# Second MLP in tiles of 128 tokens with another order of the norm; both MLPs with five up-products of 128 rows

## The reference, cut to what matters

```
x  = x + proj(attention(layernorm(x)))                       # first block
x  = x + (gelu(layernorm(x) @ mlp_w1 + mlp_b1) @ mlp_w2 + mlp_b2)

h  = irfft2(filter(rfft2(layernorm(x)))) + layernorm(x)      # second block
h  = h + x
m  = gelu(layernorm(h) @ fc1_w + fc1_b) @ fc2_w + fc2_b      # 192 -> 768 -> 192
out = m + h
```

## Time and profile before

| | |
|---|---|
| median of 3 runs | 1118.7 us (1117.19 to 1119.45) |
| profiled execution | 1113.0 us, its span 1111.2 us |
| mean granted TensorE clock | 0.959 of full |
| busy: TensorE, VectorE, ScalarE, GpSimd | 1033.5 (93%), 847.2 (76%), 700.6 (63%), 170.7 us (15%) |
| chain that ended last, by engine | PE 71%, DVE 12%, DMA 7%, ACT 5%, issue 3%, POOL 2% |
| down-products, 864 | 77.5 us busy |
| up-products, 432 | 75.0 us busy |

### The profile page before, as it was taken

One profiled execution on the slowest core, in us unless ns is written; L12 is line 12 of the kernel. 1 busy time (PEld: TensorE's weight loads), 2 busy tenths in 40 slices (PEclk: granted clock), 3 DMA queues, 4 the chain that ended last, 5 costly groups with the idle time before them and its releaser, 6 DMA issues.

```text
span 1111.2 us, 35967 instructions
## 1 busy us (share of the span) xinstructions
PE 1033.5 (93%) x15606; PEld 731.5 (66%) x15606; DVE 847.2 (76%) x1714; ACT 700.6 (63%) x1003; POOL 170.7 (15%) x142
## 2 busy tenths in 40 slices
PE   5867889999999999999999999999989889998998
PEld 3545246665777776677776767676657776775776
DVE  4837978889999999999999999999526764233443
ACT  4646157677787777777777877777865442231554
POOL 4430000910000000000000000000024544001443
PEclk9885579999999999999999999999999999999999
DMA  4698967657474756565656566554400001211110
GB/s 122 172 223 271 239 119 167 107 99 129 85 121 93 111 97 107 96 107 101 103 100 105 104 99 108 96 95 88 80 13 21 25 23 34 68 54 41 40 45 23
DMA packets 83011, 109.17 MB, mean 98 GB/s; under 512 B 14109, under 2 KB 75234, under 8 KB 82661
## 3 DMA queue, kind: packets, MB, share of 16 engines
q1 hardware_dynamic: 82853, 106.87, 48.9%
HBM read 85.40 MB, written 21.44 MB: 96 GB/s over the span
## 4 chain that ended last, share of the span: by engine, by line
PE 71%; DVE 12%; DMA 7%; ACT 5%; issue 3%; POOL 2%; SPq 0%; DVEq 0%; ACTq 0%; POOLq 0%
PE ps L1028 35%; PE ps L1189 17%; PE ps L1023 15%; DVE mx_p L1485 4%; DVE xh L101 2%; POOL rstd L109 1%; DMA m_d<-mneg 1%; DVE stage_lo L1454 1%; PE ps L1041 1%; ACT hid_f L955 1%; DVE stats L88 1%; DMA rel_d<-stage_lo 1%; DMA rel<-in_c_rel_w 1%; PE ps L1135 1%; DMA qv<-m_d 1%
## 5 line engine op out<-in xcount | busy, mean ns | idle before, releaser
L1485 DVE TENSOR_REDUCE mx_p<-ps 128x1 f32<-128x464 f32 (+1 forms) x1080 | 608.6, 629 | 34.4 <-PE ps L1028 23.2
L905 ACT ACTIVATE prob<-ps 128x768 f32<-128x768 f32 x648 | 496.2, 810 | 184.9 <-PE ps L1028 184.1
L1028 PE MATMUL ps<-kc,qc 112*32 112x464 f16 (+1 forms) x4320 | 460.4, 370 | 8.6 <-issue 4.4
L1028 PE MATMUL ps<-qv,ka 113*32 113x384 f16 x5184 | 403.8, 328 | 10.3 <-DMA qv<-m_d 7.7
L1189 PE MATMUL ps<-prob,v_ext 128*32 128x384 f32 x2592 | 293.3, 487 | 2.5 <-issue 2.0
L1028 PEld LDWEIGHTS ps<-qv,ka 113*32 113x32 f16 x5184 | 213.9, 97 | 86.7 <-issue 28.6
L1028 PEld LDWEIGHTS ps<-kc,qc 112*32 112x32 f16 x4320 | 173.2, 95 | 108.0 <-DVE mx_p L1485 30.0
L1189 PEld LDWEIGHTS ps<-prob,v_ext 128*32 128x32 f32 x2592 | 117.0, 111 | 17.4 <-issue 3.2
L1023 PE MATMUL ps<-w_dn,hid 128*96 128x192 f16 x864 | 77.5, 249 | 6.6 <-DVE hid L1540 4.4
L1023 PEld LDWEIGHTS ps<-w_dn,hid 128*96 128x96 f16 x864 | 73.2, 125 | 12.0 <-issue 6.1
L752 POOL COPY v_ext<-v_all 128x288 f32<-128x288 f32 x12 | 5.1, 427 | 480.6 <-PE ps L1189 480.5
(11 more groups left out here) (106 smaller groups left out, 838.2 us busy)
## 6 DMA issues: line engine op xcount, KB each, us to landing
qv<-rel_d SPq DMA_DIRECT2D x216, 144.0 KB
qv<-kq_d SPq DMA_DIRECT2D x108, 216.0 KB
qc<-rel_d SPq DMA_DIRECT2D x24, 216.0 KB, 4.0
xin<-in_x SPq DMA_DIRECT2D x12, 288.0 KB, 3.3
kq_d<-khl SPq DMA_DIRECT2D x24, 144.0 KB, 2.3
q_h<-kq_d SPq DMA_DIRECT2D x9, 288.0 KB, 4.7
q_w<-qw_d SPq DMA_DIRECT2D x9, 288.0 KB, 6.7
rel_d<-stage_hi SPq DMA_DIRECT2D x4, 648.0 KB, 7.6
```

The lines of the kernel that those rows point to most:

```text
L905: nc.scalar.activation(prob[:, s4(p, s), :].rearrange("p (a b) -> p a b", a=2), ps[:, 3 + 2 * (s % 2):5 + 2 * (s % 2), 0:CW], ACT.Exp).the ...
L1028: ins = nc.tensor.matmul(ps[c:c + 32, bank, 0:w], l[:, c:c + 32], r, start=True, stop=True, tile_position=(0, c))
L1485: nc.vector.tensor_reduce(mx_p[:, q * GT + k // MP, k % MP:k % MP + 1], ps[:, slot, 0:min(MW, N - k % MP * MW)], AX, ALU.max).then_inc(uni ...
```

## The change

Both MLPs: the channels are cut in 128 and 64, not 96 and 96. The high and the low part of the 64 channels are stacked in one piece of 128 rows (x[:, 2, :]), and the weight rows of these channels are loaded twice, so that two products of 128 rows (w high, w low) give all four of their combinations. An up tile is then 5 products: 3 for the 128 channels and 2 for the 64. ScalarE and VectorE each take two instructions for the parts of x instead of one. gain, shift and the weights w_up have 128 partitions; gain and shift of each norm are loaded by two DMAs, so that 4 loads come to `load_weights`, and `load_mlp` has one more load each.

Second MLP alone: `down` works in three tiles of 128 tokens (54 products) instead of four of 96 (72). x3 is written in tiles of 96 tokens, so SP stores it to memory and reads it back as x3t in tiles of 128 (`to_wide_tiles`); GpSimd adds the bias there (`bias_into_wide`), VectorE writes y_o in two instructions. The inverse transform of the next chunk comes before the up-products, the transposes before the wait for the low parts, GpSimd's rstd after two hid tiles, not four, and VectorE's two hid tiles after xh.

```diff
@@ -331,12 +336,12 @@
...
-            load(eng, gain[1][:, :], d["L0_conv_ln2_g"].rearrange("(k p) -> p k", p=C2))
-            load(eng, shift[1][:, :], d["L0_conv_ln2_b"].rearrange("(k p) -> p k", p=C2))
-            load(eng, gain[2][:, :], d["L1_conv_g2"].rearrange("(k p) -> p k", p=C2))
-            load(eng, shift[2][:, :], d["L1_conv_be2"].rearrange("(k p) -> p k", p=C2))
+            for dst, nm in ((gain[1], "L0_conv_ln2_g"), (shift[1], "L0_conv_ln2_b"),
+                            (gain[2], "L1_conv_g2"), (shift[2], "L1_conv_be2")):
+                load(eng, dst[:, 0:1], d[nm][0:128].rearrange("(p o) -> p o", o=1))
+                load(eng, dst[0:C - 128, 1:2], d[nm][128:C].rearrange("(p o) -> p o", o=1))
...
@@ -631,7 +636,9 @@
...
-                sp.dma_start(w_up_f[i][:, :, :], d[up].rearrange("(k p) n -> p k n", p=C2)).then_inc(w_mlp_in, 16)
+                sp.dma_start(w_up_f[i][:, 0, :], d[up][0:128, :]).then_inc(w_mlp_in, 16)
+                sp.dma_start(w_up_f[i][:, 1, :], d[up][128:C, :].unsqueeze(0).to_broadcast([2, C - 128, HID]))\
+                  .then_inc(w_mlp_in, 16)
...
@@ -693,15 +700,27 @@
...
+            def to_wide_tiles(c):
+                rows_c = x3_d[c * CW:(c + 1) * CW, :]
+                sp.wait_ge(x3_ok, c + 1)
+                sp.dma_start(rows_c.rearrange("(t p) c -> p t c", p=T), x1[:, ds(c * CT, CT), :]).then_inc(x3_out, 16)
+                sp.wait_ge(x3_out, 16 * (c + 1))
+                sp.dma_start(x3t[:, c % 2, :, :], rows_c.rearrange("(j p) c -> p j c", p=128))\
+                  .then_inc(x3t_in[c % 2], 16)
...
+                if more:
+                    to_wide_tiles(c + 1)
...
@@ -806,14 +825,19 @@
...
+            def bias_into_wide(c):
+                pool.wait_ge(x3t_in[c % 2], 16 * (c // 2 + 1))
+                x = x3t[:, c % 2, :, :]
+                nc.gpsimd.tensor_tensor(x, x, rows[:, 3:4, :].to_broadcast([128, 3, C]), ALU.add).then_inc(x3b_ok, 1)
+
             def block1(c, more):
-                lo_of_hidden(c, up1, range(POOL_TILES))
+                bias_into_wide(c)
+                lo_of_hidden(c, up1, range(2))
                 if more:
                     norm_root(pool, nc, rstd, ln4, c + 1)
-                    bias_into(c + 1, 3, ln4, x3b_ok)
+                lo_of_hidden(c, up1, range(2, POOL_TILES))
...
@@ -889,12 +913,14 @@
...
+                x = chunk_of(xnt_all, c)
+                for k, m in enumerate((128, C - 128)):
...
-                nc.scalar.activation(chunk_of(xnt_all, c)[:, :, 0, :], xnt_f[:, :, :], ACT.Copy).then_inc(x_hi, 1)
+                nc.scalar.activation(x[:, 0, :], xnt_f[:, 0, :], ACT.Copy)
+                nc.scalar.activation(x[0:C - 128, 2, :], xnt_f[0:C - 128, 1, :], ACT.Copy).then_inc(x_hi, 1)
...
@@ -1247,15 +1277,15 @@
...
-                    for k in range(2):
-                        for part in range(2):
-                            mm(ps[:, m % 2, 0:CW], w_up[i][:, k, part, m * 128:(m + 1) * 128], x[:, k, 0, :],
-                               start=(k == 0 and part == 0), stop=False)
+                    w, o = w_up[i][:, :, :, m * 128:(m + 1) * 128], ps[:, m % 2, 0:CW]
+                    mm(o, w[:, 0, 0, :], x[:, 0, :], stop=False)
+                    mm(o, w[:, 0, 1, :], x[:, 0, :], start=False, stop=False)
 
                 def lo_products(m):
-                    for k in range(2):
-                        ins = mm(ps[:, m % 2, 0:CW], w_up[i][:, k, 0, m * 128:(m + 1) * 128], x[:, k, 1, :],
-                                 start=False, stop=(k == 1))
+                    w, o = w_up[i][:, :, :, m * 128:(m + 1) * 128], ps[:, m % 2, 0:CW]
+                    mm(o, w[:, 0, 0, :], x[:, 1, :], start=False, stop=False)
+                    mm(o, w[:, 1, 1, :], x[:, 2, :], start=False, stop=False)
+                    ins = mm(o, w[:, 1, 0, :], x[:, 2, :], start=False)
...
@@ -1272,31 +1302,36 @@
...
+                W, late = (T, (1, 3)) if i == 0 else (128, (1,))
...
-                            mm(down_tile(t), hid[:, m, 0, t * T:(t + 1) * T], w_dn[i][:, part, m, :],
+                            mm(down_tile(t), hid[:, m, 0, t * W:(t + 1) * W], w_dn[i][:, part, m, :],
...
                 for tiles in (range(HM - 2), range(HM - 2, HM - 1), range(HM - 1, HM)):
                     pe.wait_ge(sems["hi"], c * HM + tiles.stop)
                     for t in (0, 2):
                         hi_products(t, tiles)
+                if i == 1:
+                    half_way()
                 pe.wait_ge(sems["lo"], (c + 1) * HM)
                 for t in (0, 2):
                     lo_products(t)
-                half_way()
-                for t in (1, 3):
+                if i == 0:
+                    half_way()
+                for t in late:
                     hi_products(t, range(HM))
                     ins = lo_products(t)
                 ins.then_inc(sems["dn_ps"], 1)
...
@@ -1401,7 +1436,9 @@
...
-                up(c, 1, up1, {2: lambda: inverse_w(c + 1)} if more else {})
+                if more:
+                    inverse_w(c + 1)
+                up(c, 1, up1, {})
                 down(c, 1, up1, lambda: norm_transposed(c + 1, ln4, t4_ps) if more else None)
...
@@ -1460,7 +1497,9 @@
...
-                nc.vector.tensor_tensor(x[:, :, 1, :], xnt_f[:, :, :], x[:, :, 0, :], ALU.subtract).then_inc(x_lo, 1)
+                nc.vector.tensor_tensor(x[:, 1, :], xnt_f[:, 0, :], x[:, 0, :], ALU.subtract)
+                nc.vector.tensor_tensor(x[C - 128:128, 2, :], xnt_f[0:C - 128, 1, :], x[0:C - 128, 2, :],
+                                        ALU.subtract).then_inc(x_lo, 1)
...
@@ -1589,17 +1628,27 @@
...
             def block1(c, more):
                 tiles = range(POOL_TILES, HM)
                 if more:
-                    inverse(c + 1, lambda: lo_of_hidden(c, up1, tiles))
-                else:
-                    lo_of_hidden(c, up1, tiles)
-                mlp_sum(c, up1, x3b_ok, lambda: wait_used(dve, y_out, 16 * c))
+                    inverse(c + 1, lambda: None)
+                lo_of_hidden(c, up1, tiles)
+                if more:
+                    lo_of_input(c + 1, 1)
+                dve.wait_ge(up1["dn_ps"], c + 1)
+                dve.wait_ge(x3b_ok, c + 1)
...
+                nc.vector.scalar_tensor_tensor(out=y[:, 0:2 * C], in0=ps[:, 2, 0:2 * C], scalar=1 / WS,
+                                               in1=x3[:, 0:2 * C], op0=ALU.mult, op1=ALU.add)
```

65 lines of the change are left out of this document (40 added, 25 removed).

## The result

The changed kernel takes 1138.62 us (median, 1137.73 to 1140.65), the kernel before 1117.95 us in the same session: ratio 1.0204, 95% interval 1.0170 to 1.0237. I had forecast 1118.5, so it is 20.1 us slower than forecast and above the range. The profiled execution of it took 1137.73 us with a span of 1135.9, that of before 1113.01 with 1111.2.

What follows compares the result with a forecast made beforehand. TensorE was taken to bound the second MLP, a chain through VectorE the first. The terms 1.9 - 1.7 + 1.1 + 0 - 2.3 + 0.8 = -0.2 us, added to 1118.7, gave 1118.5; range 1109 to 1125.

Steps and rivals of the forecast that it cites:

- Constants, +1.9: Second head: four more small loads in SP's queue, ahead of the qv loads, cost 1.9 us (bounds 0 and +2.5).
- The bigger w_up_f load: Beside attention: the larger up-weight load costs 0, as no row shows TensorE waiting for it.
- First MLP, -1.7: First MLP: -0.2 us for each of four rounds, chunk 0 gains 0.5, the last chunk 0.4; bounds +1.0 and -3.5.
- Start of the second MLP, +1.1: Second MLP's start: x3's store and read-back before u2's load delay the first up-product by 1.1 us; bounds 0.2 and 2.
- A steady chunk, 14.35: Second MLP: rounds of 14.35 us against 14.34, xh waiting on GpSimd instructions; 0 over five rounds, bounds -8.7 and +1.5.
- Last chunk, -2.3: Second MLP's last chunk, no norm beside it: fewer down-products give -2.1, with the two y_o instructions -2.3 us.
- Clock, +0.8: TensorE's longer waits in the first MLP and new ones in the second: half of one more half-clock stretch, +0.8 us.
- rival C: Second MLP: half-clock stretches of 3.3 us after TensorE's new wait, 1.7 us each, +4.1 in all, 1122.8; chance 0.17.
- A: Second MLP: TensorE and ScalarE bound throughout, the lock hurts little, rounds of 12.6 us, -9.7 in all, 1109; chance 0.13.
- B: Second MLP: x3's round trip lasts past 9.1 us, so the bias misses xh; rounds of 13.35, -6.0, 1112.7; chance 0.15.
- D: Second head: the constants cost nothing, SP's delay being absorbed; -2.1 us in all, 1116.6; chance 0.10.

Runs made afterwards that it cites:

- e2: e1 with the four short gain and shift loads moved from the second head to the sixth; 1127.95 us, ratio 1.0083 to the kernel before.
- e1: The changed kernel with the one broadcast transfer of up-weight rows 128 to 192 written as two plain transfers of 64 rows; 1132.09 us, ratio 1.0124.
- e8: The kernel before plus one broadcast transfer of up-weight rows in the first head, into a tile nobody reads; 1120.33 us, ratio 1.0051.
- e9: e4 with the first MLP of the kernel before; 1109.62 us, ratio 0.9922.
- e5: e4 with the first product of each up tile in the first MLP run twice; 1117.26 us, ratio 1.0016.
- e10: e4 with short loads spread over heads 4 to 7; in the first MLP's last chunk GpSimd's tiles after xh, VectorE's before h; 1111.60 us, ratio 0.9960.
- e12: e1 with ten products nobody reads in TensorE's wait for xh in each second-MLP chunk; 1126.42 us, ratio 1.0078.
- e11: e10 with products nobody reads in TensorE's waits of the first MLP; 1105.00 us, ratio 0.9894.
- e4: e1 with the second MLP in the order of before, 128-token tiles kept, and three hid tiles each on GpSimd and VectorE; 1117.41 us, ratio 0.9989.

## Why the prediction was wrong, step by step

*Constants, +1.9.* The mechanism held, the size was 3.9 in the profile and 4.1 by e2. The row of issues grew by 2.9, not 1.9, TensorE's wait by 2.4, and the half clock behind that wait makes up the rest; I had counted four issues alone.

*The bigger w_up_f load, "lies beside attention; no row shows TensorE waiting for it, taken 0".* This is the step that failed most: the first head is 11.1 us longer, 2.4 of it by half-clock stretches behind the new waits (reckoned as below). I looked for who waits for that load, and nobody does. What it holds up are the small transfers behind it on the same engines, and the earlier trace rows had shown TensorE waiting for just such a one, m_d. e1 and e8 show that the transfer is the cause; that it goes over two engines is read from its packets, 2.1 under way at a time, and that its outermost dimension of 2 is the reason rests on e1, where the same bytes as two transfers of 64 rows go over all 16. The Trainium skill says it outright (DMA: Bandwidth & Descriptors, "Rules for kernel authors"): an outermost dimension below 16, "e.g. a leading zero-stride broadcast of c copies", confines a transfer to at most c engines. The trace agrees, and I had not held the new line of the diff against that rule.

*First MLP, -1.7.* It became +7.3. For the rounds between chunks I had -0.2 each. Where no half clock lies in them or ahead of them they are level with before (19.59 us against 19.48): y_sb and rstd come 0.37 us later by the doubled rounding (I had 0.2), and what the tiles gain on GpSimd doesn't reach the chain. The five rounds grew by 1.8 because 6.83 us of them stand at half clock instead of 3.41. Chunk 0 gained nothing, since its round stayed 17.33. The last chunk, for which I had -0.4, lost 5.5, because I had not followed VectorE there: xh, h and the skip sum stand ahead of tiles 4 and 5, and nothing else fills TensorE. Of these 5.5 only 1.0 to 1.5 are the change's own delay; 2.5 are the half clock behind the wait, and the rest is that the stretch of before lay ahead of this chunk and brought it forward by as much as it had cost. Taking each round and chunk as it is where no stretch lies in it or ahead of it, I estimate the whole at 111.6 us before (17.37, 20.12, three of 19.48, and e9's 15.68) and 113.4 after (17.33, 20.57, three of 19.59, and 16.72, with half of what TensorE worked in the two stretches taken off the second round and the last chunk): some 1.8 of the 7.3 are the change's own and 5.2 its two stretches of 6.83 us. e5 acquits the count of products, e9 and e10 hold the order and, by what is left, the second rounding.

*Start of the second MLP, +1.1.* Measured +1.0. TensorE waits 0.54 us for u_sb and then computes the inverse transform ahead of its first up-product, where before it waited 0.89 us for ScalarE.

*A steady chunk, 14.35.* Measured 14.61 without half clock: the lock between GpSimd and VectorE works as described, with xh at 3.79 (forecast 3.2 to 3.6), the bias started 0.04 us before tile 3 had ended, and the wait for xh at 1.80. In the last of the five rounds I had forgotten that no inverse transform is left to do: 13.32 in e1, 1.3 less. With it the five rounds would take 71.8 us at full clock (four of 14.61 and one of 13.32), 71.7 before: the forecast of 0 was right, and the 5.0 us of the table are the clock's.

*Last chunk, -2.3.* From 1121.75 to VectorE's start at 1132.37 are 10.62 us; 12.95 before; so -2.3. Down products 54 in 4.62.

*Clock, +0.8.* This term failed as badly as the load's, and it was rival C in full, and more. Three stretches of 3.41 us in the second MLP at 1.65 each, two of 6.83 us instead of one of 3.41 around the first, and three in the first two heads after the new waits. The earlier trace rows had shown that a stretch follows waits; I weighed that against the neighbouring chunks without one and gave it 0.17. Ten waits of 1.8 to 7.5 us are new or longer (three in the heads, two in the first MLP, five in the second), and eight stretches begin in them or just behind. They are not beside the places above but inside them. TensorE works 35.1 us in these eight and 6.8 in the two of before; if each costs half of that, which is an estimate and holds where TensorE is the bound (in the second MLP it gives 5.1, as e12 measured), they are worth 17.5 and 3.4 us, so some 14 of the 24.7 us between the profiles. e12 and e11 show that filling the wait keeps the clock, although the round stays as long as the wait made it.

The rivals: A's mechanism was false for the change and true once the order and the split of the tiles were turned (e4). B didn't occur; x3t was there when the bias started, 7.8 us into the round. D was the wrong way round.

## What to carry to other kernels

Read every new DMA for its outermost dimension, and ask what small transfer stands behind it, not only who waits for its data. When TensorE gets less work in a stage whose order has VectorE and GpSimd side by side, follow both through the first and the last round too, where the collisions differ from the steady one. A wait that is added costs twice where the clock falls behind it (1.8 us and then 1.65 in three rounds of five here); in the second MLP products that nobody reads, as long as the wait, gave the second half back. And before two profiles are compared chunk by chunk, see where the half-clock stretches lie in each: one of them ahead of a chunk changed its wait by 1.5 to 1.9 us, and it can pay back in the next chunk what it cost in its own.

## What the runs showed of the hardware that I had not expected

- A transfer of 384 KB that goes over two of the 16 DMA engines takes from 166 to 182 us and holds up what is queued behind it: the qv loads until 188 us, 1.5 KB by 8.4 us instead of 1.2, and SP itself for 8.41 us over three issues.
- From attention on the half clock comes in stretches of 3.41 or 6.83 us and costs about half of each (1.65 of 3.41 in the second MLP); in the first MLP, whose round is a chain through VectorE, the next chunk gave 1.4 to 1.9 us of it back. It moves from chunk to chunk between runs of the same code (in the first MLP of before: fifth round in before and e8, third in e9), so it is priced as a number of stretches, not at a place.
- A few tenths of a us in when xh starts change which GpSimd instruction lies on which VectorE one. In the last chunk of the first MLP xh takes 1.84 us when it starts 2.91 us after the first up-product and 2.56 at 3.36 (code of before); 3.08 at 2.97 and 4.45 at 3.70 (changed code). The earlier start stands wherever a half-clock stretch lies in the round ahead; in the fourth chunk of e9, behind its stretch, xh again starts at 2.91 and takes 1.84.
